# Last stage of a four-stage kernel: results added by the scatter's DMA; semaphores zeroed a stage later; first attention without its loop

## What is computed

```python
def _L1_ffn_ref(hidden_states, norm_weight, router_w, sw1, sb1, sw2, sb2, ew1, eb1, ew2, eb2):
    ...
    shared = jnp.maximum(normed @ sw1 + sb1, 0.0) @ sw2 + sb2
    ...
    scores, idx = jax.lax.top_k(probs, TOPK)
    w = scores / (jnp.sum(scores, axis=-1, keepdims=True) + 1e-06)
    ...
    h = jnp.maximum(jnp.einsum('td,edh->teh', flat, ew1) + eb1[None, :, :], 0.0)
    eo = jnp.einsum('teh,eho->teo', h, ew2) + eb2[None, :, :]
    routed = jnp.einsum('teo,te->to', eo, comb)
    return shared + routed.reshape(b, s, -1)
...
x = x + _L1_ffn_ref(_layernorm(x, axis=-1), ...)
```

## Time and profile before

| | us |
|---|---|
| median of three runs | 1531.55 |
| lowest and highest | 1527.78, 1532.58 |
| the profiled execution | 1531.16 |
| its span in the trace | 1529.3 |
| first attention, up to its barrier | 273.4 |
| second stage (experts) | 276.5 to 703.5 |
| third stage (attention) | 706.9 to 1158.9 |
| last stage | 1162.7 to 1524.9 |
| zeroing of semaphores after it | to 1529.2 |

### The profile page before, as it was taken

The page is one execution under the profiler, slowest core; times in us unless marked ns, Lnnn a source line. Parts: engine busy times, 40 slices in busy tenths (PEclk is TensorE's granted clock), DMA queues, the critical chain, the costliest instruction groups (busy, mean ns, idle before and its releaser), DMA issues. The chain is left out here.

```text
span 1529.3 us, 36918 instructions
## 1 busy us (share of the span) xinstructions
PE 1274.5 (83%) x13441; PEld 1052.8 (69%) x13441; DVE 1012.4 (66%) x2018; ACT 889.1 (58%) x1661; POOL 619.6 (41%) x680
## 2 busy tenths in 40 slices
PE   4888888299999999994899999999962767799980
PEld 3777776178777787783798888988851555577760
DVE  5888887566777668763356676666754765476662
ACT  3777777466566666653455666556632455577750
POOL 3222221145555555563223232332220665067771
PEclk9999999599999999997899999999985587799995
DMA  4222221332221322122100000000001221136746
GB/s 139 91 86 87 88 87 56 112 90 77 83 63 49 90 77 70 49 76 79 46 9 16 9 17 9 16 9 9 2 2 48 85 68 36 44 103 216 217 152 175
DMA packets 90357, 108.59 MB, mean 71 GB/s; under 512 B 15594, under 2 KB 57194, under 8 KB 90218
## 3 DMA queue, kind: packets, MB, share of 16 engines
q1 hardware_dynamic: 80906, 80.73, 17.7%
q0 software_dynamic: 9312, 26.03, 4.9%
HBM read 61.11 MB, written 29.82 MB: 59 GB/s over the span
## 5 line engine op out<-in xcount | busy, mean ns | idle before, releaser
L813 POOL TENSOR_TENSOR b_h_lo<-b_h,b_h_hi 128x512 fp32r<-128x512 f32 x168 | 216.5, 1293 | 179.9 <-ACT b_h_hi L837 179.4
L832 ACT ACTIVATE b_zg<-b_zg 128x512 f32<-128x512 f32 x168 | 97.6, 581 | 81.4 <-PE b_zg L876 81.2
L837 ACT ACTIVATE b_h_hi<-b_h 128x512 fp32r<-128x512 f32 x168 | 105.1, 626 | 67.0 <-DVE b_h L1041 66.8
L1041 DVE TENSOR_TENSOR b_h<-b_zg,b_uw 128x512 f32<-128x512 f32 x168 | 116.2, 691 | 32.0 <-ACT b_zg L832 26.7
L1916 POOL DMA_INDIRECT planes_dram<-d_y_out,d_back x92 | 96.3, 1046 | 80.9 <-DVE d_y_out L2224 58.9
L1034 DVE TENSOR_TENSOR b_uw<-b_zu,b_gw 128x512 f32<-128x512 f32 x128 | 88.2, 689 | 58.2 <-PE b_zu L876 51.0
L2193 DVE TENSOR_TENSOR d_h_lo<-d_h,d_h_hi 128x512 fp32r<-128x512 f32 x124 | 84.0, 696 | 37.5 <-ACT d_h_hi L1954 17.6
L1579 DVE TENSOR_TENSOR c_oT_lo<-c_oy,c_oT_hi 128x512 fp32r<-128x512 f32 x64 | 44.1, 689 | 94.1 <-ACT c_oT_hi L1323 94.1
L1240 POOL TENSOR_TENSOR c_prob<-c_prob,c_recip 128x512 f32<-128x512 f32 x64 | 65.4, 1043 | 99.3 <-DVE c_recip L1572 99.3
L314 POOL TENSOR_TENSOR a_qx<-a_qT,headmask 128x256 f32<-128x256 f32 x64 | 37.9, 613 | 147.0 <-ACT a_qT L349 147.0
L1229 POOL TENSOR_TENSOR c_c_hi<-c_craw,c_zero 128x256 fp32r<-128x256 f32 x32 | 19.7, 614 | 170.5 <-issue 164.2
(11 more groups left out here) (354 smaller groups left out, 4171.8 us busy)
## 6 DMA issues: line engine op xcount, KB each, us to landing
rows_dram<-a_blank SPq DMA_DIRECT2D x32, 520.0 KB
b_gw<-gates_dram SPq DMA_DIRECT2D x64, 256.0 KB, 3.8
d_up_slot<-d_up_tab POOLq DMA_DIRECT2D x15, 512.0 KB
d_down_slot<-d_down_tab POOLq DMA_DIRECT2D x15, 512.0 KB
d_xg<-rows_dram SPq DMA_DIRECT2D x23, 260.0 KB
b_gm<-gates_dram SPq DMA_DIRECT2D x32, 160.0 KB, 4.0
c_craw<-in_c_ctxT_dram SPq DMA_DIRECT2D x16, 256.0 KB, 2.9
d_pay<-planes_dram SPq DMA_DIRECT2D x16, 256.0 KB, 4.6
```

Source lines behind the costliest of these rows:

```text
L813: pool.tensor_tensor(h_lo[:, m % HS, :], h[:, m % HF, :], h_hi[:, m % HS, :].bitcast(F32), ALU.subtract).then_inc(lo_done.sem, 1)
L832: act.activation(zg_ps[:, n % ZG, :], zg_ps[:, n % ZG, :], ACT.Silu).then_inc(sg_done.sem, 1)
L837: act.activation(h_hi[:, m % HS, :], h[:, m % HF, :], ACT.Copy).then_inc(hi_done.sem, 1)
L1041: dve.tensor_tensor(h[:, n % HF, :], zg_ps[:, n % ZG, :], uw[:, n % 2, :], ALU.mult).then_inc(h_done.sem, 1)
```

## The change

Three edits, of which only the first touches what the DMAs move.

1. In the last stage the results are added in DRAM. There is one plane, `sums_dram`, of 4096 rows and 512 spare ones. When a group's shared result is in `x`, SP stores the group of `x` to it (semaphore `begun`; the spare rows get a copy too, nine stores in all), in jobs 3 to 10. POOL's scatter has `compute_op=ALU.add`: the DMA adds to the rows. Since two tiles can now hit one row, POOL waits before each tile's four scatters until the four of the tile before have landed (one semaphore `added`), and before the first tile for the nine stores. At the end SP copies `sums_dram` to the output in eight DMAs, DRAM to DRAM. Fetching and adding planes is gone.
2. A stage's semaphores are zeroed by PE at the start of the next stage; the zeroing block and its barrier are gone, except at the very end, where SP still zeroes the last stage's 61.
3. `pipeline` writes out all 36 steps; the loop and its register arithmetic are gone.

```diff
+class Earlier:
+    def clear(self, eng):
+        for s in self.sems:
+            eng.sem_clear(s)
+    def replace(self, sems, held):
+        self.held.close()
+        self.sems, self.held = sems, held
...
-        with nc.Block() as block:
-            @block.sync
-            def _(sp):
-                for s in taken:
-                    sp.sem_clear(s)
+        earlier.replace(taken, held)
...
-    for t in range(depth):
-        step(lambda lag, t=t: At(t // width, t % width, lag, width), lambda lag, t=t: t - lag >= 0)
-    with eng.Fori(depth // width, units // width) as k:
-        for j in range(width):
-            step(lambda lag, j=j: At(k, j, lag, width), lambda lag: True)
-    for t in range(units, units + depth):
-        step(lambda lag, t=t: At(t // width, t % width, lag, width), lambda lag, t=t: t - lag < units)
+    for t in range(units + depth):
+        step(lambda lag, t=t: At(t // width, t % width, lag, width), lambda lag, t=t: 0 <= t - lag < units)
...
         @block.tensor
         def _(pe):
+            earlier.clear(pe)
...
+                if 0 <= k - 3 < GROUPS:
+                    j = k - 3
+                    sp.wait_ge(out_done.sem, out_done.at(j + 1))
+                    for first in (j * COLS, B * N)[:2 if j == 0 else 1]:
+                        sp.dma_start(results[first:first + COLS, :].rearrange("(u p) f -> p u f", p=P),
+                                     x[:, j * GROUP:(j + 1) * GROUP, :]).then_inc(begun, 16)
...
-            for s in range(2):
-                sp.wait_ge(added[s], 16 * GROUP * ((TILES + 1 - s) // 2))
...
-            for g in range(PAY):
-                fetch(g)
+            sp.wait_ge(added, 16 * GROUP * TILES)
             for g in range(GROUPS):
-                sp.wait_ge(summed.sem, summed.at(2 * g + 2))
-                if g + PAY < GROUPS:
-                    fetch(g + PAY)
-                sp.dma_start(out[g * COLS:(g + 1) * COLS, :].rearrange("(u p) f -> p u f", p=P),
-                             x[:, g * GROUP:(g + 1) * GROUP, :]).then_inc(stored, 16)
+                sp.dma_start(out[g * COLS:(g + 1) * COLS, :], results[g * COLS:(g + 1) * COLS, :]).then_inc(stored, 16)
...
+                    if t == 0:
+                        pool.wait_ge(begun, 16 * (GROUPS + 1))
+                    else:
+                        pool.wait_ge(added, 16 * GROUP * t)
                     for u in range(GROUP):
                         pool.indirect_dma_start(
-                            planes, bass.IndirectOffsetOnAxis(ap=back[:, t, u:u + 1], axis=0),
-                            y_out[:, t % 2, u, :], None).then_inc(added[t % 2], 16)
+                            results, bass.IndirectOffsetOnAxis(ap=back[:, t, u:u + 1], axis=0),
+                            y_out[:, t % 2, u, :], None, compute_op=ALU.add).then_inc(added, 16)
...
                         if t >= 2:
-                            dve.wait_ge(added[t % 2], 16 * GROUP * (t // 2))
+                            dve.wait_ge(added, 16 * GROUP * (t - 1))
...
-            for g in range(GROUPS):
-                tiles = x[:, g * GROUP:(g + 1) * GROUP, :]
-                dve.wait_ge(fetched[g % PAY], 32 * (g // PAY + 1))
-                for n in range(2):
-                    dve.tensor_tensor(tiles, tiles, pay[:, g % PAY, n, :, 0:C], ALU.add).then_inc(summed.sem, 1)
```

More of the change, by code:

```diff
@@ L75, in chunk_plan, with __init__, stage @@
     return plan
+class Earlier:
+    def __init__(self):
+        self.sems, self.held = [], ExitStack()
+    def clear(self, eng):
[4 more added lines that the diff above has]
+        self.sems, self.held = sems, held
 @contextmanager
-def stage(nc):
+def stage(nc, earlier):
     with ExitStack() as ctx:
-        taken = []
-        ctx.sem = lambda name: taken.append(ctx.enter_context(nc.semaphore(name))) or taken[-1]
+        taken, held = [], ExitStack()
+        ctx.sem = lambda name: taken.append(held.enter_context(nc.semaphore(name))) or taken[-1]
         with ExitStack() as blocks:
@@ L182, in finish_stats, with attention0 @@
     return vector, scalar, ready
-def attention0(nc, x, stats, ident, headmask, x_in, w_qkvT, w_projT, b_proj, ctx_kT, ctx_v, consts,
+def attention0(nc, earlier, x, stats, ident, headmask, x_in, w_qkvT, w_projT, b_proj, ctx_kT, ctx_v, consts,
                rows):
-    with stage(nc) as ctx:
+    with stage(nc, earlier) as ctx:
         def sb(name, shape, dt=F32):
@@ L499, in step @@
                     scores(new)
[L501 removed]
+            pipeline(UNITS, DEPTH, step, 4)
         @block.vector
@@ L1075, in _, with attention1 @@
                         dve.bn_stats(stats[:, g * GROUP + i, :], x[:, g * GROUP + i, :])
-def attention1(nc, x, stats, ident, a):
-    with stage(nc) as ctx:
+def attention1(nc, earlier, x, stats, ident, a):
+    with stage(nc, earlier) as ctx:
         def sb(name, shape, dt=F32):
@@ L1650, in _, with sorted_experts @@
                 tops(n + 1)
-def sorted_experts(nc, x, stats, ident, a, rows, planes, out):
+def sorted_experts(nc, earlier, x, stats, ident, a, rows, results, out):
     tag = "d_"
@@ L2236, in _, with program @@
             ticks(step)
-            for g in range(GROUPS):
-                tiles = x[:, g * GROUP:(g + 1) * GROUP, :]
-                dve.wait_ge(fetched[g % PAY], 32 * (g // PAY + 1))
-                for n in range(2):
-                    dve.tensor_tensor(tiles, tiles, pay[:, g % PAY, n, :, 0:C], ALU.add).then_inc(summed.sem, 1)
-                    if n == 0:
-                        dve.wait_ge(summed.sem, summed.at(2 * g + 1))
-def program(nc, a, rows, gates, planes, out):
+def program(nc, a, rows, gates, sums, out):
     with ExitStack() as ctx:
+        earlier = Earlier()
         x = ctx.enter_context(nc.sbuf_tensor("x_resid", [P, UNITS, C], F32))
@@ L2251, in program, with _ @@
         headmask = ctx.enter_context(nc.sbuf_tensor("headmask", [P, FOUR], F32))
-        attention0(nc, x, stats, ident, headmask, a["x"], a["a_wqkvT"], a["a_wprojT"], a["a_bproj"],
+        attention0(nc, earlier, x, stats, ident, headmask, a["x"], a["a_wqkvT"], a["a_wprojT"], a["a_bproj"],
                    a["a_ctx_kT"], a["a_ctx_v"], a, rows)
-        experts(nc, x, stats, ident, a, gates)
-        attention1(nc, x, stats, ident, a)
-        sorted_experts(nc, x, stats, ident, a, rows, planes, out)
+        experts(nc, earlier, x, stats, ident, a, gates)
+        attention1(nc, earlier, x, stats, ident, a)
+        sorted_experts(nc, earlier, x, stats, ident, a, rows, sums, out)
+        with nc.Block() as block:
+            @block.sync
+            def _(sp):
+                earlier.clear(sp)
+        earlier.replace([], ExitStack())
 def layout(inp):
```

37 lines of the change are left out of this document (15 added, 22 removed).

## The result

| | us |
|---|---|
| before, median | 1529.66 |
| after, median | 1561.74 |
| ratio after / before | 1.0206, 95% interval 1.0165 to 1.0247 |
| the profiled execution after | 1555.45 (span 1553.7) |

The account below looks back on a forecast made before the run. PE was taken to bound the first attention and last-stage tile jobs, DMA the last 26 us. 1531.2 - 10.3 - 0.2 - 5.0 - 14.6 + 7.4 + 1.0 = 1509.5 us, range 1500 to 1527.

Parts of the forecast that it names:

- The scatter as a chain: Last stage: each tile's scatters wait for the tile before; just fits the jobs' 7.30 us, costing +7.4 us at the end.
- P: Least time a tile's turn takes in the last stage's scatters: 6.57 us without adding's extra cost, 7.27 as taken.
- x: Time by which adding lengthens a scatter's landing, as the DMA reads the row first; taken 0.7 us, ends 0 and 1.27.
- y: Time adding puts on POOL for each scatter, four a tile; taken 0 us, ends 0 and 0.3.
- rival 2: Last stage: the adding scatters' chain outweighs all gains; turn of 9.04 us, +47.2, kernel 1549 us; chance 0.13.
- The condition written down for being wrong: Last stage: a scatter takes 1.2 us on POOL or lands over 3 us after its start.
- The wake: Last stage: POOL starts a scatter 0.28 us after what it waited for.
- Boundaries: Between stages: three zeroing blocks gone, -10.3 us, with PE's zeroings covered by its idle time.
- The loop: First attention: seven loop turns -3.7 us and register instructions -1.3, together -5.0, between -3.7 and -6.8.
- The end: After the last landing: eight DRAM to DRAM copies take 11.0 us in place of 25.6, -14.6, between -6.3 and -17.9.
- SP's stores: Last stage: SP's wait in job 3 delays a weight load, so ACT may wait 0 to 2.5 us; taken +1.0.
- Rival 3: Written-out first attention stalls on instruction loading, or PE's zeroings aren't covered; 1517.5 us, chance 0.10.

Follow-up runs that it names:

- no_add_chained: The changed kernel with all its waits, but the scatter overwrites rows in place of adding; 1493.11 us, ratio 0.9823 against the kernel before.
- the half width: The changed kernel with each adding scatter moving 128 half rows of 256 bytes; 1556.96 us, ratio 1.0184 against the kernel before.
- unrolled_only: The kernel before with only the written-out `pipeline` of the changed one; 1519.88 us against 1529.13, ratio 0.994.
- before_again: The kernel before, unchanged, profiled once more; 1530.68 us.
- plain_scatter: The changed kernel with the last stage as before: two planes, plain scatter, the old end; 1500.73 us against 1519.55, ratio 0.9884.
- zeroed_later_only: The kernel before with only the semaphore zeroing moved to PE at the next stage's start; 1521.11 us, ratio 0.9943.
- plain_2kb: The changed kernel with plain scatter and old end, planes' rows renumbered so final fetches move 2 KB pieces; 1509.84 us against 1529.13, ratio 0.9865.

## Why the prediction was wrong

**The scatter as a chain: the step that failed is y.** The form P = 4.06 + 2.23 + 0.28 + x + 4y holds; it reaches 7.27 with the terms taken and 9.68 with those measured:

| term | taken | measured | from |
|---|---|---|---|
| first to last scatter, plain | 4.06 | 3.79 | 1468.86 - 1465.07 in `no_add_chained` |
| landing, plain | 2.23 | 2.23 | `no_add_chained` |
| POOL after the landing | 0.28 | 0.77 | 1471.86 - 1468.86 - 2.23 |
| x | 0.7 | 0.49 | 3.32 - 2.23 - 0.60 |
| y, four times | 0 | 0.60 | 1.56 - 0.96 |

A turn in the last tiles takes 9.64. The step "I take x = 0.7 and y = 0, since only one more read is in the way and the rows are small" put the price of adding into the DMA, and there it was right within 0.2 us. But the price lies mostly on the engine that issues: four times 0.60 is 2.4 us a tile, which is the whole difference between 7.27 and 9.68 (the other three terms together are right, by errors that cancel: -0.27, +0.49, -0.21), and the jobs' 7.30 left only 0.73 us over the plain chain. The argument from small rows is what the half width refutes: bytes don't matter to POOL. Its upper end of 0.3 was also too low, being half the time of a copy, an operation of another kind. With x and y at the upper ends rival 2 gave P = 9.04 and 1549 us; it is the rival that came, with a larger P and at 0.13 of the chance. The condition written down for being wrong (over 1.2 us on POOL, landing over 3 us) is met in both halves.

The page of the Trainium skill named in rival 2 (Collectives: The Full Stack, "Why ReduceScatter is half of AllGather") speaks of the reduction between cores in a collective. It pointed in this direction, but no run here shows descriptors or that rate. The runs show more packets for an adding scatter, 128 where there were 16, at the same number of counted bytes; POOL's time grows by a factor of 1.63 and the landing by 1.5, so neither doubles.

**The wake.** The 0.28 us were read between DVE's end and POOL's start, not behind a DMA's landing: there it is 0.77. As the time from a tile's first scatter to its last was over-read (4.06, with the longer scatters of busy tiles, where the last tiles have 3.79), the plain chain came out only 0.22 us short, 6.57 against 6.79.

**The way to the jobs.** That the jobs slow down to P once it exceeds 7.30 is right. The prediction let this go through DVE's wait for a buffer alone, and had the copies of weights lie inside the wait for the landing. The trace shows that wait only three times while PE still works (0.60, 3.58 and 0.91 us); in the 15 tiles whose weights are copied PE starts as soon as the copy can have landed, because POOL issues the copies behind a scatter that is late.

**The steady part.** P = 9.97 on average, 0.3 above the last tiles: there a tile's scatters start within 5.57 us, in the busy tiles mostly within 5.7 to 6.1, with single scatters of up to 2.07 us. By the prediction's own form this gives 23 x 9.97 - 0.28 = 229.0 us from first scatter to last landing; it was 228.2.

**Boundaries: right.** 10.3 us, and PE's 149 zeroings (0.06 us each by their own duration; 42 of them from 265.7 to 270.6, 0.12 each) are hidden: PE's first work stands 272.49 - 265.5 = 7.0 us behind the barrier, 7.2 before, and the only other engine that waits for them is ACT, once, for 0.3 us.

**The loop: right in kind, too small.** -7.9 (after) and -8.5 (`unrolled_only` against `before_again`), where -5.0 was predicted and -6.8 was the upper end. The turn's 0.53 us times seven hold, 3.7 us. The mis-sized term is that of the registers: a unit takes 7.35 us in place of 7.50, so 28 x 0.15 = 4.2 us, where 1.3 was taken. It was priced by three instructions on PE alone; which engine's instructions make up the rest wasn't tried. The Trainium skill (Advanced Engine Details and Errata, Control Flow Timing) gives about 108 ns for a compare-and-branch. No engine's branch in the loop before shows that: PE's median is 208 ns, those of SP, POOL and ACT 45 and that of DVE 56.

**The end: right, a little better.** 9.3 us where 11.0 was taken: the eight copies move 2.1 MB in it at 228 GB/s, near the 242 assumed, but issue and landing lie inside these 9.3 us and not, with 2.3 us, beside them.

**SP's stores: no cost.** The weight loads do leave later, as predicted, but the routing part, from the last stage's barrier to the first scatter, isn't longer for it. On the faster chip it takes 165.4, 165.8 and 165.9 us in the three kernels with the stores and 166.1 in `plain_scatter` without them. On the others it takes 169.3 (the changed kernel), 174.0, 172.8, 173.4 and 172.7 with them and 176.1 (the kernel before), 175.6, 175.9, 176.5 and 175.8 without. So 4.7 of the -6.8 of the table above are the spread from execution to execution (the changed kernel itself has 169.3 and 174.0). The 2 to 3 us that are left can't be put down to the first edit: apart from the first value of each list, which have no chip on record, the kernels with the stores all ran on one chip and those without on another.

**Rival 3** (instruction loading, uncovered zeroings): nothing of it showed, in `unrolled_only`, `zeroed_later_only` or `plain_scatter`.

## What to carry to other kernels

Letting an indirect DMA add has to be priced first on the engine that issues it, once for each DMA, and only then on the DMA; rows of half the bytes made it no cheaper there. Then look at what stands behind it in that engine's stream, as the copies of weights did here. When work is turned into a chain, list every term of a turn from rows of the same kind (a wake behind a landing from a landing, not from another engine's semaphore), and where the most numerous term is shown by no row, as the four times y was here, its lack of a row has to widen the range. Saving 16 us at the end of a kernel isn't worth 2.7 us in each of 22 turns.

## What the runs showed of the hardware

- An adding indirect DMA of 128 rows takes 1.56 us on POOL where a plain one takes 0.96, and the next indirect DMA starts 0.30 us behind that. Some 0.4 us of the difference are fixed and 1.4 ns go by the row (64 and 128 rows); rows of 256 in place of 512 bytes change nothing. A direct DMA behind it starts after 0.99 us already.
- It has one packet for each row, 128 for a scatter, where the plain one has 16 (from the counts 19616, 13728 and 9312, if nothing else in the queue changed).
- POOL's direct copies of weights, which have nothing to do with the adding, take 1.18 us in every kernel whose scatters add (1.12 where they take 64 rows) and 0.58 to 0.60 in every one where they don't, chained or not. They start 0.58 us apart in both. Why is open.
- Behind a landed DMA POOL's next indirect DMA starts 0.76 us later, 0.69 of it as issue.
- A copy from DRAM to DRAM of 2.1 MB in 16 KB pieces ends 9.3 us after the last landing.
- The last stage's routing part is 3 to 10 us longer on some chips than on one. On the former ACT stands in it, two to eight times and 8 to 23 us in all, with the releaser given as remote; on the latter no kernel shows such a wait. What it waits for stays open. The longest in `plain_2kb`, timeline of ACT:

```profile
1242.98 0.69 ACT L1955 ACTIVATE d_h<-d_z,d_b_tab 128x512 f32<-128x512 f32 x1 [5.87 <-remote]
```
